# A block of mixing, attention and eight experts: the second norm before the router's ranking, one token tile scaled on VectorE, four slots for hidden tiles

## The chip, the cores and the metric

The kernel runs on one core of a Trainium2 chip. The metric is the device time in microseconds (us) of one execution; the figure for a kernel is the median of its runs. Engines: TensorE (PE; PEld is its weight load), VectorE (DVE), ScalarE (ACT), GpSimd (POOL), SyncE (SP, which only issues DMAs here).

## What is computed

For each of 8 batches: an attention-free mixing layer over 256 image tokens, 128 embedded text tokens appended, relative-position attention over all 384 tokens, then 8 experts weighted by a router. The reference, cut to what matters here:

```python
h = tok_mix(x)                    # h = (h - mu) * rsqrt(var + 1e-5) * ln_g + ln_b at its end
h = jnp.concatenate([h, W_E[x_txt] * sqrt(256)], axis=1)          # 256 + 128 tokens of 256
h = h + attn(_layernorm(h))       # 16 heads of 16, relative positions in a window of 4
x2 = _layernorm(h)
inh = sigmoid(x2 @ Wr / temperature)                              # router, 8 experts
w = exp(-dist / 0.1) * in_zone                                    # dist = |inh - 1/e|
fb = exp(-dist / 0.3); fb_w = normalise(fb * (fb is one of the two largest))
w = normalise(where(sum(w) < 1e-8, fb_w, w))
hidden = silu(x2 @ Wg[e]) * (x2 @ Wu[e])                          # 256 wide, each expert e
out = h + sum_e w[e] * (hidden @ Wd[e])
```

## The kernel before

**Tiles and loop.** Tokens stand on the 128 partitions: three tiles of 128 tokens (two of the image, one of the text), 256 values each. The experts of batch b-1 run in the same iteration as the mixing and the attention of batch b. The first iteration (batch 0) has no experts, seven iterations (six in a loop, one written out after it) have both, and a last pass has the experts of batch 7 alone.

**The order of the work.** `schedule` (line 332) writes out one list of steps, and each engine runs the part that it has in each step, in that order; engines wait for each other with counting semaphores only. So a step that waits on an engine holds up all that stands behind it on that engine. The steps of the mixing and the attention are fixed; between them `fill(n)` puts the next n *units* of the experts, TensorE work of batch b-1. `FILL_MIX` (line 80) says after which step of the mix how many units follow, `FILL_MAXIMA` the same for the 24 maxima (one unit after every third), `FILL_NEGATE` (3 units) for the second negation of the maxima, `FILL_OUT` for the steps behind attention.

**Units.** Gate G(n) and up U(n), n = 0 to 15, two per expert, are six matmuls of 128x384 each (line 913) into one PSUM bank each. ScalarE makes silu of G(n) (line 1070), VectorE multiplies it by U(n) into the hidden tile H(n) (line 1362); U(n+1) may start only when H(n) has freed the bank, and the silu of G(n+1) only when H(n) has read the one before. The hidden tiles have three slots: H(n) goes to slot n mod 3 and waits for the down product that last read it. The down product D(e) of expert e has two parts (line 934): token tiles 0 and 1, then tile 2; VectorE accumulates them, weighted by the router, as A(e) (line 1374), three instructions. The next expert's part waits for the accumulation of the same tiles. H and A don't follow their unit at once on VectorE: each is written just ahead of the next unit, so behind whatever steps lie between.

The units were listed G0 U0 G1 U1, then per expert e: G and U of slot 2e+2, D(e), G and U of slot 2e+3. D(e) has therefore one hidden tile in hand beyond those it reads.

**The mix's end.** The steps in order, with their units: `residual`, `mix_in`, `turn_x2`, `mix_sums`, `router` G0, `mix_out`, `router_zone` U0, `mix_norm` G1, `router_rank` U1 G2, `norm_stats` U2 D0 (first part), `router_pick` D0 (second), `turn_norm` G3 U3, `project_qk`, `project_rel` G4, `project_v` and 15 more units, up to D3.

- `mix_norm`: VectorE normalises the two image tiles out of PSUM into `hid` (line 1115); GpSimd multiplies each by `ln_g` and adds `ln_b` (lines 1439, 1441), tile 0 and then tile 1, counting `hid_ready`.
- `router_rank`, `router_pick`: VectorE, 5 and 11 small instructions, each of which waits for the one before (lines 1331 to 1335, 1341 to 1353).
- `norm_stats`: VectorE waits for `hid_ready` to reach 5 (text tile 1, image tiles 2 each), then takes statistics of the three tiles (lines 1104, 1109); GpSimd's `root` (lines 1405, 1408) turns the variance into 1/sqrt.
- `turn_norm`: VectorE normalises (line 1115, `scratch<-hid`), TensorE transposes (line 658), ScalarE copies (line 977). `project_qk` (line 741) waits for that. Afterwards GpSimd adds a bias to all of `hid` (line 1451).
- From `project_qk` on, ScalarE and VectorE split queries and keys into three bfloat16 parts; SP sends them through DRAM and back in stacked form (lines 561, 566), and last fetches the skewed relative logits as `band_t` (line 595). The first of the maxima (lines 779, 787, reduced on VectorE at line 1220) waits for `band_t`, through a copy on VectorE (line 1214).

**Behind the mix.** The maxima are negated in two halves: TensorE transposes into the bank that tile 2 of a down product also uses, so it waits for the accumulations before it; then attention (scores line 827, band added by VectorE line 1241, exponential by ScalarE line 1033, values line 844). ScalarE loads its table anew between silu and exponential. After attention, `turn_outputs` and `turn_attn`, then `turn_weights`: VectorE scales the relative weights (line 1261), TensorE transposes them (line 658).

## Time and profile before

| | us |
|---|---|
| runs of the kernel before: median (lowest to highest of 3) | 1249.13 (1246.06 to 1252.84) |
| the profiled execution: its own time | 1249.12 |
| its span in the profile | 1247.3 |
| TensorE busy | 1020.4 |
| VectorE busy | 753.0 |
| ScalarE busy | 451.2 |
| GpSimd busy | 247.8 |

The span runs from the first to the last instruction recorded. Busy time counts matmuls as pipelined, with ends that are modelled. "Idle before" in a timeline is the time that the engine did nothing ahead of an instruction, with the instruction that ended last among those it waited for. Times in a timeline are us from the start of the span. The rows are of the iteration whose mix ends at about 490 us; the others of the seven repeat it.

### The profile page before, as it was taken

The numbers are of one execution on the slowest core, as the hardware profiler recorded it, in microseconds if no ns is written. First come the engines' busy times: TensorE is split into PE (matmuls) and PEld (weight loads), VectorE is DVE, ScalarE is ACT, GpSimd is POOL, SyncE is SP. The second block draws the span as 40 slices with busy tenths as digits, with TensorE's granted clock in tenths as the row PEclk, the third lists the DMA queues.
The fourth block names the chain that finished last, engine by engine and source line by source line (L and its number), as shares of the span: only waits on it lengthen the run. The fifth ranks groups of instructions, "written<-read, shape, count | busy, mean of one in ns | idle before, by whom it ended". The sixth has DMA issues, their size and how long they took to land.

```text
span 1247.3 us, 16776 instructions
## 1 busy us (share of the span) xinstructions
PE 1020.4 (82%) x5668; PEld 744.4 (60%) x5668; DVE 753.0 (60%) x1597; ACT 451.2 (36%) x651; POOL 247.8 (20%) x262
## 2 busy tenths in 40 slices
PE   3536698888898798888898798988988888987798
PEld 2412277636786287745786377854876367862687
DVE  7347355774648755685658745685567746487343
ACT  1133512453124723355124622346224531347211
POOL 6228411021200402013200412004120212004000
PEclk9569789989999999999999999999999999999899
DMA  4286203602062110802044020722026020620100
GB/s 110 101 240 174 68 5 97 140 11 53 4 178 59 24 42 33 202 10 39 18 121 115 9 56 0 202 44 39 18 79 157 10 52 5 179 60 18 35 1 13
DMA packets 96962, 87.87 MB, mean 70 GB/s; under 512 B 67281, under 2 KB 85074, under 8 KB 95090
## 3 DMA queue, kind: packets, MB, share of 16 engines
q1 hardware_dynamic: 96524, 86.24, 28.3%
q0 software_dynamic: 384, 1.05, 0.3%
q8 instruction: 17, 0.28, 0.1%
q14 instruction: 37, 0.30, 0.1%
HBM read 60.35 MB, written 26.92 MB: 70 GB/s over the span
## 4 chain that ended last, share of the span: by engine, by line
PE 46%; issue 22%; DVE 17%; DMA 5%; ACT 4%; POOL 4%; SPq 2%; POOLq 0%; DVEq 0%; ACTq 0%
PE S L913 16%; PE S L934 8%; DVE maxima L1220 4%; PE S L844 4%; PE S L779 4%; PE S L827 4%; PE S L741 3%; DVE S L1241 3%; ACT scratch L1033 3%; PE S L658 1%; DMA txt_row<-in_L_txt_W_E,txt_idx 1%; DVE res L1374 1%; PE S L760 1%; SPq L566 1%; PE S L787 1%
## 5 line engine op out<-in xcount | busy, mean ns | idle before, releaser
L1491 POOL TENSOR_TENSOR bands<-scratch,one 64x432 f32<-64x432 f32 x128 | 119.1, 931 | 525.0 <-ACT scratch L1033 519.4
L1070 ACT ACTIVATE silu<-S 128x384 f32<-128x384 f32 x128 | 63.0, 492 | 352.2 <-PE S L913 243.6
L1220 DVE TENSOR_REDUCE maxima<-S 128x2 f32<-128x768 f32 x192 | 172.2, 951 | 19.0 <-PE S L787 17.6
L934 PE MATMUL S<-w_d,hT 128*128 128x256 f32 x768 | 182.0, 382 | 1.5 <-DVE hT L1362 0.7
L1241 DVE TENSOR_TENSOR S<-S,bands 64x144 f32<-64x144 f32 x384 | 154.3, 402 | 43.3 <-PE S L827 32.6
L1033 ACT ACTIVATE scratch<-S 128x768 f32<-128x768 f32 x192 | 154.8, 812 | 56.3 <-DVE S L1241 43.0
L779 PE MATMUL S<-k_st,q_st 128*128 128x384 bf16 x384 | 101.9, 334 | 68.0 <-DVE maxima L1220 39.7
L934 PEld LDWEIGHTS S<-w_d,hT 128*128 128x128 f32 x768 | 143.4, 191 | 22.2 <-issue 2.3
L1362 DVE TENSOR_TENSOR hT<-silu,S 128x384 f32<-128x384 f32 x128 | 70.7, 552 | 116.7 <-PE S L913 97.4
L827 PE MATMUL S<-q_st,k_st 128*128 128x384 bf16 x384 | 98.8, 356 | 40.2 <-ACT scratch L1033 36.7
L1011 ACT ACTIVATE scratch<-scratch 128x816 bf16<-128x816 bf16 x56 | 92.3, 1694 | 41.5 <-DMA scratch<-d_band_t 41.5
L779 PEld LDWEIGHTS S<-k_st,q_st 128*128 128x128 bf16 x384 | 37.6, 98 | 116.3 <-DVE maxima L1220 58.0
L1374 DVE SCALAR_TENSOR_TENSOR res<-S,wgt,res 128x256 f32<-128x256 f32 x168 | 75.5, 479 | 48.0 <-PE S L934 47.7
L827 PEld LDWEIGHTS S<-q_st,k_st 128*128 128x128 bf16 x384 | 25.6, 99 | 132.1 <-ACT scratch L1033 104.0
L844 PE MATMUL S<-scratch,v_one 128*17 128x384 f32 x768 | 84.0, 522 | 12.4 <-ACT scratch L1033 12.3
L913 PE MATMUL S<-x_hi,wu_hi 128*128 128x384 f32 x256 | 72.1, 363 | 23.7 <-DVE hT L1362 23.7
L787 PE MATMUL S<-scratch,ident_b 128*128 128x132 bf16 (+1 forms) x384 | 85.7, 224 | 0.0
L913 PE MATMUL S<-x_hi,wg_hi 128*128 128x384 f32 x256 | 78.1, 386 | 0.0
L658 PE MATMUL S<-ident,scratch 128*128 128x128 f32 (+1 forms) x196 | 30.2, 294 | 51.5 <-DVE scratch L1115 29.9
L913 PE MATMUL S<-x_lo,wu_hi 128*128 128x384 f32 x256 | 66.4, 341 | 0.0
L913 PE MATMUL S<-x_hi,wg_lo 128*128 128x384 f32 x256 | 66.4, 341 | 0.0
L913 PE MATMUL S<-x_lo,wg_hi 128*128 128x384 f32 x256 | 66.3, 340 | 0.0
(167 smaller groups left out, 1515.6 us busy)
## 6 DMA issues: line engine op xcount, KB each, us to landing
bands<-d_band_s SPq DMA_DIRECT2D x16, 864.0 KB, 9.4
scratch<-d_band_t SPq DMA_DIRECT2D x8, 1632.0 KB, 9.6
d_parts<-scratch SPq DMA_DIRECT2D x48, 192.0 KB, 1.9
q_st<-d_parts SPq DMA_DIRECT2D x48, 192.0 KB
k_st<-d_parts SPq DMA_DIRECT2D x48, 192.0 KB
d_band_w<-bands SPq DMA_DIRECT2D x32, 240.0 KB, 3.9
out<-scratch SPq DMA_DIRECT2D x8, 384.0 KB, 2.6
x_in<-in_x SPq DMA_DIRECT2D x8, 256.0 KB, 3.6
```

The source lines that it names most:

```text
L779: pe.matmul(S[:, bank, PAD:PAD + T], q_st[:, h, i * P:(i + 1) * P], k_st[:, h, :], start=True, stop=False, skip_group_check=True)
L787: mm = pe.matmul(S[rows, bank, at + w0:at + w1], ident_b[rows, rows], band_h[rows, i, h, w0:w1], start=False, stop=True, skip_group_check= ...
L827: mm = pe.matmul(S[:, 2 * (n % 3) + l, PAD:PAD + T], k_st[:, h, i * P:(i + 1) * P], q_st[:, h, :], start=True, stop=True)
L844: mm = pe.matmul(S[32 * l:32 * l + VC, 6 + g % 2, 0:T], v_one[:, i, h, :], p_t[:, h % PTS, i, :], start=(i == VALUE_TILES[0]), stop=(i == ...
L913: mm = pe.matmul(dst[:, 0:T], ws[:, e, k, m * P:(m + 1) * P], xs[:, k, :], start=(j == 0), stop=(j == 3 * KT - 1))
L934: mm = pe.matmul(D[:, i // 2, (i % 2) * E:(i % 2 + 1) * E], hT[:, (FT * e + m) % 3, i * P:(i + 1) * P], w_d[:, e, m, :], start=(m == 0), s ...
L1011: nc.scalar.activation(band_h[:, :, heads], band_t[:, :, :, heads].rearrange("p i w h -> p i h w"), ACT.Copy).then_inc(band_turned.sem, 1)
L1033: nc.scalar.activation(dst, S[:, c0:c0 + 2, PAD:PAD + T], ACT.Exp).then_inc(exp_done.sem, 1)
L1220: dve.tensor_reduce(dst, S[:, c0:c0 + 2, PAD:PAD + T], AX, ALU.max).then_inc(max_done.sem, 1)
L1241: dve.tensor_tensor(win, win, band, ALU.add).then_inc(sc_add.sem, 1)
L1374: dve.scalar_tensor_tensor((out_st if last else res)[:, i], D[:, i // 2, (i % 2) * E:(i % 2 + 1) * E], wgt[:, i, e:e + 1], res[:, i], ALU. ...
L1491: nc.gpsimd.tensor_tensor(bands[rows, :, :, 2 * pair:2 * pair + 2].rearrange("p i w h -> p h i w"), win, one[rows].unsqueeze(2).unsqueeze( ...
```

## The change

The steps at the mix's end become: `mix_norm` G1, `norm_stats` U1 G2 U2, `turn_norm` G3, `router_rank` U3, `router_order`, `router_pick` D0 (both parts), `project_qk`, `project_rel` G4 U4, `project_v` and 14 more units. `router_rank` keeps its first two instructions, `router_order` is the other three. Image tile 1 is multiplied by `ln_g` and has `ln_b` added on VectorE, right behind the normalisation; GpSimd does tile 0 alone. The hidden tiles have four slots, and four pairs of gate and up come ahead of the first down product; then per expert D(e) and two pairs. So the units behind `project_v` end with U9 instead of D3, and the units between the maxima are, in order, the parts of D3, G10, U10, G11, U11 and the parts of D4, where they were G9, U9, G10, U10, the parts of D4, G11, U11. The units at the second negation are G12 U12 G13 instead of G12 U12 and the first part of D5. Behind attention come U13, D5, G14, U14, G15, U15, D6, and D7 with its first part after the relative weights are turned; before, the order was the second part of D5, G13, U13, G14, U14, D6, G15, U15, and then D7 likewise.

```diff
...
@@ -78,9 +79,9 @@
-            ("mix_out", 0), ("router_zone", 1), ("mix_norm", 1), ("router_rank", 2),
-            ("norm_stats", 2), ("router_pick", 1), ("turn_norm", 2), ("project_qk", 0),
-            ("project_rel", 1), ("project_v", 15)]
+            ("mix_out", 0), ("router_zone", 1), ("mix_norm", 1), ("norm_stats", 3), ("turn_norm", 1),
+            ("router_rank", 1), ("router_order", 0), ("router_pick", 2), ("project_qk", 0),
+            ("project_rel", 2), ("project_v", 14)]
@@ -168,7 +169,7 @@
-        hT = sb("hT", [P, 3, T])
+        hT = sb("hT", [P, HSLOTS, T])
@@ -266,7 +267,7 @@
-        hid_ready = sig("hid_ready", 5)
+        hid_ready, hid_second = sig("hid_ready", 3), sig("hid_second", 2)
@@ -315,13 +316,15 @@
-        units = [("gate", 0), ("up", 0), ("gate", 1), ("up", 1)]
+        units = []
+        for n in range(HSLOTS):
+            units += [("gate", n), ("up", n)]
         for e in range(NE):
-            if e + 1 < NE:
-                units += [("gate", 2 * e + 2), ("up", 2 * e + 2)]
-            units += [("down", e, 0), ("down", e, 1)]
-            if e + 1 < NE:
-                units += [("gate", 2 * e + 3), ("up", 2 * e + 3)]
+            parts_e = [("down", e, 0), ("down", e, 1)]
+            n = FT * e + HSLOTS
+            if n < FT * NE:
+                parts_e += [("gate", n), ("up", n), ("gate", n + 1), ("up", n + 1)]
+            units += parts_e
...
@@ -932,7 +935,7 @@
-                                       hT[:, (FT * e + m) % 3, i * P:(i + 1) * P], w_d[:, e, m, :],
+                                       hT[:, (FT * e + m) % HSLOTS, i * P:(i + 1) * P], w_d[:, e, m, :],
@@ -1147,6 +1150,13 @@
             def mix_norm(b):
                 norm(b, mix_dve, mix_root, mixed, lambda i: hid[:, i], IT)
+                if not later(b):
+                    dve.wait_ge(loaded[1], 16 * N_LOADS[1])
+                dve.wait_ge(mix_dve.sem, mix_dve.at(b, 5 + 3 * IT))
+                dve.tensor_tensor(hid[:, 1], hid[:, 1], ln_g[:], ALU.mult).then_inc(hid_second.sem, 1)
+                dve.wait_ge(hid_second.sem, hid_second.at(b, 1))
+                dve.tensor_tensor(hid[:, 1], hid[:, 1], ln_b[:], ALU.add).then_inc(hid_second.sem, 1)
@@ -1179,7 +1189,8 @@
             def norm_stats(b):
-                dve.wait_ge(hid_ready.sem, hid_ready.at(b, 5))
+                dve.wait_ge(hid_ready.sem, hid_ready.at(b, 3))
+                dve.wait_ge(hid_second.sem, hid_second.at(b, 2))
                 stats(b, ln2, 0, lambda i: hid[:, i], TT)
@@ -1330,6 +1341,12 @@
                 low = earlier[:].unsqueeze(1).broadcast_to([P, TT, NE, NE])
                 step(dve.tensor_tensor(rpair, other, own, ALU.is_equal))
                 step(dve.tensor_tensor(rpair, rpair, low, ALU.mult))
+            def router_order(b):
+                step = stepper(b, [R_DIST + 7])
+                other = fb.unsqueeze(2).broadcast_to([P, TT, NE, NE])
+                own = fb.unsqueeze(3).broadcast_to([P, TT, NE, NE])
                 step(dve.tensor_tensor(rpair, rpair, rpair2, ALU.add))
                 step(dve.tensor_reduce(rank, rpair, AX, ALU.add))
@@ -1356,10 +1373,10 @@
             def hidden(f, n):
-                if n >= 3:
-                    dve.wait_ge(down_pe.sem, down_pe.at(f, 2 * ((n - 3) // FT + 1)))
-                dve.tensor_tensor(hT[:, n % 3], silu[:], U[:, 0:T], ALU.mult).then_inc(h_done.sem, 1)
+                if n >= HSLOTS:
+                    dve.wait_ge(down_pe.sem, down_pe.at(f, 2 * ((n - HSLOTS) // FT + 1)))
+                dve.tensor_tensor(hT[:, n % HSLOTS], silu[:], U[:, 0:T], ALU.mult).then_inc(h_done.sem, 1)
...
@@ -1412,7 +1429,7 @@
             def mix_in(b):
                 if later(b):
-                    pool.wait_ge(hid_ready.sem, hid_ready.at(b - 1, 5))
+                    pool.wait_ge(hid_ready.sem, hid_ready.at(b - 1, 3))
@@ -1434,11 +1451,10 @@
-                for i in range(IT):
-                    pool.wait_ge(mix_dve.sem, mix_dve.at(b, 5 + 2 * IT + 1 + i))
-                    nc.gpsimd.tensor_tensor(hid[:, i], hid[:, i], ln_g[:], ALU.mult).then_inc(hid_ready.sem, 1)
-                    pool.wait_ge(hid_ready.sem, hid_ready.at(b, 2 + 2 * i))
-                    nc.gpsimd.tensor_tensor(hid[:, i], hid[:, i], ln_b[:], ALU.add).then_inc(hid_ready.sem, 1)
+                pool.wait_ge(mix_dve.sem, mix_dve.at(b, 5 + 2 * IT + 1))
+                nc.gpsimd.tensor_tensor(hid[:, 0], hid[:, 0], ln_g[:], ALU.mult).then_inc(hid_ready.sem, 1)
+                pool.wait_ge(hid_ready.sem, hid_ready.at(b, 2))
+                nc.gpsimd.tensor_tensor(hid[:, 0], hid[:, 0], ln_b[:], ALU.add).then_inc(hid_ready.sem, 1)
             def norm_stats(b):
```

`HSLOTS` is 4. The hunks left out enter `router_order` in the lists of steps.

## Rows read from the trace of the kernel before

**Rows 1.** The page: span; busy time by engine

```profile
span 1247.3 us, 16776 instructions
...
PE 1020.4 (82%) x5668; PEld 744.4 (60%) x5668; DVE 753.0 (60%) x1597; ACT 451.2 (36%) x651; POOL 247.8 (20%) x262
```

**Rows 2.** Waits of TensorE, whole run: us in total, times, longest us

```profile
PE S L913 <- DVE hT L1362: 23.7, 15, 2.6
```

**Rows 3.** TensorE, one iteration: start us, us, line, tiles [idle before <-releaser]

```profile
476.44 0.62 PE L913 MATMUL S<-x_hi,wu_hi 128*128 128x384 f32 x2 [1.54 <-DVE hT L1362]
...
480.30 0.62 PE L913 MATMUL S<-x_hi,wu_hi 128*128 128x384 f32 x2 [1.49 <-DVE hT L1362]
...
486.27 0.88 PE L658 MATMUL S<-ident,scratch 128*128 128x128 f32 x6 [2.06 <-DVE scratch L1115]
...
489.10 2.74 PE L741 MATMUL S<-scratch,w_q 128*128 128x384 f32 x8
```

**Rows 4.** Timeline of VectorE, same iteration

```profile
475.84 0.54 DVE L1362 TENSOR_TENSOR hT<-silu,S 128x384 f32<-128x384 f32 x1
...
480.16 1.07 DVE L1104 BATCH_NORM_STATS2 stat<-hid 128x6 f32<-128x256 f32 x3
...
485.16 1.05 DVE L1115 TENSOR_SCALAR scratch<-hid,mv,rstd 128x256 f32<-128x256 f32 x3
```

**Rows 5.** Timeline of GpSimd (POOL), same iteration

```profile
475.55 0.72 POOL L1439 TENSOR_TENSOR hid<-hid,ln_g 128x256 f32<-128x256 f32 x1 [0.66 <-DVE hid L1115]
...
476.35 0.90 POOL L1441 TENSOR_TENSOR hid<-hid,ln_b 128x256 f32<-128x256 f32 x1
...
486.29 1.87 POOL L1451 TENSOR_TENSOR hid<-hid,bo_all 128x768 f32<-128x768 f32 x1 [3.49 <-DVE scratch L1115]
```

**Rows 6.** Two lines of VectorE, whole run: ns min/median/max

```profile
L1332 DVE TENSOR_TENSOR scratch<-scratch,earlier x8: 358/784/787, 186.5 to 1187.5; 128x192 f32<-128x192 f32 x8
...
L1206 DVE TENSOR_TENSOR v_one<-S,bv_all x24: 411/416/420, 65.5 to 1073.3; 128x256 f32<-128x256 f32 x24
```

**Rows 7.** Timelines of ScalarE and TensorE where the first maxima wait

```profile
516.78 1.67 ACT L1011 ACTIVATE scratch<-scratch 128x816 bf16<-128x816 bf16 x1 [3.10 <-DMA scratch<-d_band_t]
...
517.97 0.34 PE L779 MATMUL S<-k_st,q_st 128*128 128x384 bf16 x1 [1.18 <-DVE scratch L1214]
```

**Rows 8.** Chain that ended last, maxima pass: start us, us, what

```profile
523.49 1.10 PE S L913 x6
...
533.17 1.78 PE S L934 x8
...
544.95 0.49 PE S L658 x3
```

**Rows 9.** Timeline of ScalarE, end of the maxima, first exponential

```profile
547.05 1.28 ACT L1033 ACT_TABLE_LOAD   x1
...
551.09 1.67 ACT L1033 ACTIVATE scratch<-S 128x768 f32<-128x768 f32 x2 [2.76 <-DVE S L1241]
```

**Rows 10.** Timelines of VectorE and TensorE, end of the iteration

```profile
585.88 1.35 DVE L1374 SCALAR_TENSOR_TENSOR res<-S,wgt,res 128x256 f32<-128x256 f32 x3 [1.12 <-PE S L934]
...
588.65 0.82 PE L658 MATMUL S<-ident,scratch 128*72 128x128 f32 x6
```

**Rows 11.** Timeline of TensorE, last pass

```profile
1191.78 0.82 PE L913 MATMUL S<-x_hi,wu_hi 128*128 128x384 f32 x2 [2.60 <-DVE hT L1362]
...
1240.96 2.86 PE L934 MATMUL S<-w_d,hT 128*128 128x256 f32 x12 [0.70 <-DVE hT L1362]
```

**Rows 12.** Busy us by stretch; last three columns: granted clock, DMA share, GB/s

```profile
486.30:490.00 3.70, 3.70 (x21) 3.37 (x22) 0.30 (x1) 1.37 (x3) 1.86 (x1) 1.00 0.00 0
...
1191.80:1197.00 5.20, 5.20 (x19) 4.64 (x19) 1.08 (x3) 0.49 (x1) 0.00 (x0) 0.67 0.00 0
```

**Rows 13.** Timeline of VectorE, first iteration

```profile
47.40 1.08 DVE L1104 BATCH_NORM_STATS2 stat<-hid 128x6 f32<-128x256 f32 x3 [2.73 <-POOL hid L1441]
...
50.09 1.06 DVE L1115 TENSOR_SCALAR scratch<-hid,mv,rstd 128x256 f32<-128x256 f32 x3 [1.26 <-POOL rstd L1408]
```

More of the change, by code:

```diff
@@ L37 @@
 KT = E // P
+HSLOTS = 4
 TXT = 128
@@ L357, in schedule @@
                 fill(3)
-                steps += [("router_zone",), ("router_rank",), ("router_pick",)]
+                steps += [("router_zone",), ("router_rank",), ("router_order",), ("router_pick",)]
                 fill(len(left))
@@ L414, in schedule @@
             return steps
-        LATE_STEPS = ("residual", "turn_x2", "router", "router_zone", "router_rank", "router_pick",
+        LATE_STEPS = ("residual", "turn_x2", "router", "router_zone", "router_rank", "router_order", "router_pick",
                       "gate", "up", "down", "hidden", "accumulate", "store")
@@ L1383, in _ @@
                          "turn_x2": turn_x2, "router": router, "router_zone": router_zone,
-                         "router_rank": router_rank, "router_pick": router_pick,
+                         "router_rank": router_rank, "router_order": router_order, "router_pick": router_pick,
                          "hidden": hidden, "accumulate": accumulate})
```

## The prediction

> **What bounds the kernel now.** The page comes first: the span is 1247.3 us and TensorE is busy for 82% of it [rows 1], so the time is TensorE's work and the gaps in it. The profiled execution took 1249.12 us, 1.8 more than its span; the median of the three runs is 1249.13, so a difference worked out on the trace is added to 1249.1 as it is. The table of waits says which gaps the change aims at: TensorE waited 23.7 us, in 15 places, for a hidden tile of VectorE [rows 2], two places in each of the seven iterations in which the experts of one batch run beside the mixing and attention of the next, and one in the last pass. TensorE's own timeline of one such iteration shows them: 1.54 us before U1 (the up product of slot 1) and 1.49 before U2, then 2.06 before the transposes of the normalised tokens [rows 3], 5.09 in all. VectorE's timeline shows why: H0 and H1, the products that free TensorE's bank, stand behind the router's ranking, and the second norm, at 485.16, does too [rows 4].
>
> What ends a gap is not yet what ends the stage. The projections, at 489.10 [rows 3], start a chain of DMAs whose last, the bands, lands at 516.78; TensorE has been idle for 1.18 us when the first maxima start at 517.97 [rows 7]. So that stage is set by the DMA chain, and only what brings the projections forward shortens it.
>
> **The stage of the mix, part by part.** The first norm ends on VectorE just before 475.84, where H0 starts now [rows 4]. Two instructions are put in between, a multiplication and an addition over 128x256. Alone each should take 0.42 (the nearest row of that size, with one operand in PSUM) [rows 6]. But GpSimd multiplies and adds the other tile at that moment, from 475.55 on [rows 5], and VectorE's two-operand instruction of 128x192, 0.36 at its fastest, has a median of 0.78 [rows 6]; the fastest is the last pass, where GpSimd is idle. So I let the two take turns: the multiplication waits until about 476.1, GpSimd's addition is pushed and done at about 477.0, VectorE's addition ends at 477.4. H0 starts there, 1.56 later than now, U1, which follows H0 by 0.60 [rows 3, 4], at 478.0, and the gap before it grows from 1.54 to 3.1. The bounds: 0.9 later if the engines do not hinder each other, 1.9 if each waits for the whole of the other's instruction.
>
> That last bound is a rule of the Trainium skill (SBUF — State Buffer, section "Who interferes with whom"): an instruction of VectorE with both inputs in SBUF and one of GpSimd that reads SBUF exclude each other, and whichever starts first keeps the shared ports for its whole length. The trace bears out the turns; read to the letter the rule would put H0 at 477.7 and add about 2 us to the forecast over seven iterations.
>
> What this buys: GpSimd now ends its tile at about 477.15 and no longer does the second, so the statistics, at 480.16 now [rows 4], start behind H0 at 477.9. The norm follows its statistics by 2.69 where nothing else is in the way [rows 13], so it starts at 480.6 and ends at 481.65, for 485.16 plus 1.05 [rows 4]. TensorE from U1 to the projections takes 489.10 - 476.44 = 12.66 now, of which 1.49 and 2.06 are gaps [rows 3]; about 0.5 more are tails of matmuls that overlap the next one where no gap follows (estimate), which leaves 8.6. The units in that stretch are the same after the change. From 478.0 that is 486.6, and 0.3 is still lost, as U2 is through at 481.3 and the norm at 481.65. The projections start at 486.9, **2.2 us earlier** (1.8 to 2.8 by the bounds above).
>
> The ranking and the picking move behind H2. Their steps cost nothing there as long as something covers them: they wait for GpSimd's 1.87 (the bias added to the hidden state) [rows 5] and end at about 488, with H3 and the first accumulation behind them on VectorE; H3 is wanted by U4 at about 494.6 and VectorE by the splitting of the queries at about 491. If they took 3 us more, each further microsecond would delay that splitting, and so SP's whole chain of DMAs. No DMA is added. SP's issues stay in order and move with the projections; GpSimd's gather of text rows waits for a count that is long reached. The fourth slot and the split of the ranking in two cost no instruction.
>
> **What is late next.** The bands land at 514.6 instead of 516.78. TensorE is there earlier still, since D3 (the down product of expert 3, first part 1.78 [rows 8]) leaves this stretch and G9 and U9 (1.10 each [rows 8]) come in: its gap grows, nothing is gained beyond 2.2. D3 turns up in the maxima pass, between whose reductions a unit is put every third item. There the order becomes D3, D3, G10, U10, G11, U11, D4, D4 for G9, U9, G10, U10, D4, D4, G11, U11. TensorE's unit sits in the loop from one reduction to the next, so a first down part costs 1.78 - 1.10 = 0.68 more than a gate: 0.68 for D3's, 0.68 for D4's at its new place, and -0.30 where D4's was (VectorE, with H10 and a negation there, doesn't let all of it go). The second parts are short, but two accumulations, 0.45 each [rows 10], push the reduction after them: +0.26 for D3's, -0.17 for D4's old place. Last, D4 now ends the pass, and the second negation, at 544.95 [rows 8], needs D4's bank: after the last reduction all three accumulations, 1.35, come first: +1.13. Together 0.68 + 0.68 - 0.30 + 0.26 - 0.17 + 1.13 = **+2.3**.
>
> After the negation G13 (1.10) stands in place of D5's first part (1.78), and no accumulation holds VectorE when attention starts. But G13's activation comes ahead of ScalarE's table load of 1.28 [rows 9], so the first exponential, at 551.09 [rows 9], comes only **0.5 earlier** than the negation alone would have it.
>
> Behind attention the 0.68 is paid back (+0.6), and D6 now runs directly ahead of the turned relative weights: VectorE makes these after D6's first accumulations, which it begins 1.9 after D6 starts, while now they are made under G15 and U15, with the transposes at 588.65 behind them [rows 10]: +0.7 of wait, less 0.4 for H15, which no longer delays D7. **+0.9.**
>
> **The sum without the clock.** Per iteration -2.2 + 2.3 - 0.5 + 0.9 = +0.5, seven times +3.5. The first iteration has no experts: there GpSimd's four instructions stand alone in front of the statistics (2.73 idle [rows 13]), and two of them leave: -1.1. In the last pass the 0.70 before the last down product [rows 11] goes, but D7 then waits for D6's accumulations: -0.4. Sum +2.0: 1251.1.
>
> **The clock.** TensorE ran at full clock (1.00) behind the gap of 2.06, and at 0.67 of it on average, partly at 1.2 GHz, in the 5.2 us behind the gap of 2.60 of the last pass [rows 3, 11, 12]. The new gap of 3.1 is longer than that. A fall would make U1 to U2 slower: in the last pass 5.2 us at 0.67 lost about 1.7, of which the 0.3 that TensorE waits anyway is free, and not all of a fall need meet work: 1.2 per fall (estimate). It may come in none of the iterations (0, if the gap stays near 2.4, the lower bound) or in all seven (+8.4). The one gap of this size was followed by a fall, but it was one; I take half, **+4** (3.5 x 1.2). The forecast is 1249.1 + 2.0 + 4.0 = **1255**, 0.5% above, which is about what a measurement of this kernel can tell from no change.
>
> **The rivals.** *Slower by more (chance 0.39).* The wait on H0 takes the place of those removed: the clock falls behind the 3.1 us gap in every iteration, and U1, G2 and U2 run on the slow clock. For it: [rows 11, 12]; against it: it needs the gap to stay above some 2.5 us. Time: 1251.1 + 8.4 = 1259.5; with a second fall behind the longer gap ahead of the maxima, in half the iterations, some 1264. It decides from about 5 falls in seven. The Trainium skill (TensorE: Matmul & The Clock Gate, section "What's actually happening") has the throttled clock as the default that activity releases; the trace agrees with its 0.67, and by that rule alone the time would be that of this rival.
>
> *Faster (0.18).* The maxima pass absorbs D3 and D4, because its reductions on VectorE and not the units on TensorE set its pace, and the three accumulations fit ahead of the negation: then +2.3 is about 0.5, and each iteration comes to -2.2 + 0.5 - 0.5 + 0.9 = -1.3. Time: 1249.1 - 9.1 - 1.5 = 1238.5. Against it: in the chain that ended last the units stand between the reductions [rows 8]. It decides once the pass grows by less than 1.2.
>
> *No contention (part of the middle 0.43).* VectorE's two instructions take 0.84 beside GpSimd, the gap is 2.4, the clock stays: 1251.1 - 7 x 0.6 = 1247, the same as before within what can be told.
>
> **How the numbers follow.** Within 0.5% (1242.9 to 1255.4) lie the sum without the clock, up to three or four falls, and the case without contention: 0.43. Above it the first rival, 0.39; below it the second, 0.18. The forecast lies at the upper edge of the middle case. The range 1238 to 1264 reaches to both rivals and leaves out a tenth on either side.
>
> **What would show it.** TensorE's gap before U1 at about 3.1, none before U2, 0.3 before the transposes; VectorE's two new instructions at 0.5 to 0.9 instead of 0.42; GpSimd with two fewer per iteration; the projections 2.2 earlier against the same iteration's first norm; the maxima pass, from the first maxima to the second negation, 26.98 now [rows 7, 8], at about 29.2; stretches of granted clock 0.5 behind U1 in some iterations. The prediction is wrong if H0 starts before 476.9 or if the maxima pass does not grow.

## The result and the profile after

The changed kernel took 1267.24 us (median; 1265.54 to 1268.73) against 1249.32 of the kernel before in the same comparison: a ratio of 1.0136, with a 95% interval of 1.0106 to 1.0166. It is slower by 1.4%, where 1255 was forecast and 1264 was the upper end of the range.

The page of the kernel after, its span, busy time and the row of the bands' transfer (the last number is the median from issue to landing; the same row of the kernel before has 9.6):

```profile
span 1263.5 us, 16772 instructions
...
PE 1033.3 (82%) x5668; PEld 758.4 (60%) x5668; DVE 756.5 (60%) x1613; ACT 449.7 (36%) x651; POOL 234.6 (19%) x246
...
scratch<-d_band_t SPq DMA_DIRECT2D x8, 1632.0 KB, 10.4
```

Against [rows 1] the span grew by 16.2 us, and TensorE's busy time by 12.9 with the same 5668 instructions: the same work ran on a lower clock for longer (mean 0.939 for 0.952). GpSimd (POOL) has 16 instructions fewer, two for each batch, and VectorE 16 more, as the change says. The bands, which the prediction left alone, take 0.8 us longer to land.

TensorE's waits after (us in total, times, longest us):

```profile
PE S L916 <- DVE hT L1379: 22.0, 8, 3.2
...
PE S L661 <- DVE scratch L1272: 9.4, 8, 6.7
PE S L661 <- DVE res L1391: 8.2, 6, 1.4
```

The wait for a hidden tile came 15 times for 23.7 us [rows 2]; it comes 8 times for 22.0 now: in six of seven iterations one wait of about 3 us has taken the place of two of 1.5. The two rows below it are waits of the new order of units: the relative weights wait behind D6's accumulations (seven times; the eighth, of 6.7, was there before, as 6.5), and the second negation behind D4's.

TensorE in the mix of one iteration after, the one of the fifth batch, to be read beside [rows 3]:

```profile
622.25 0.51 PE L916 MATMUL S<-x_hi,wg_lo 128*128 128x384 f32 x2
625.80 1.01 PE L916 MATMUL S<-x_hi,wu_hi 128*128 128x384 f32 x2 [3.05 <-DVE hT L1379]
626.61 0.84 PE L916 MATMUL S<-x_lo,wu_hi 128*128 128x384 f32 x2
...
631.73 0.82 PE L661 MATMUL S<-ident,scratch 128*128 128x128 f32 x6
...
637.09 2.74 PE L744 MATMUL S<-scratch,w_q 128*128 128x384 f32 x8
```

The gap before U1 is 3.05, and behind it a pair of matmuls takes 0.84 where it took 0.51 before the gap. The gaps before U2 and before the transposes are gone here. The second is gone only because TensorE is so slow that VectorE is always done first: in the iteration whose clock stays whole at this place, U2 follows G2 without a gap too, and 0.21 us is left before the transposes:

```profile
189.75 0.87 PE L661 MATMUL S<-ident,scratch 128*128 128x128 f32 x6 [0.21 <-DVE scratch L1118]
```

VectorE at the same place, beside [rows 4]:

```profile
622.79 0.99 DVE L1118 TENSOR_SCALAR hid<-S,mv,rstd 128x256 f32<-128x256 f32 x2 [0.63 <-POOL rstd L1425]
623.82 0.60 DVE L1157 TENSOR_TENSOR hid<-hid,ln_g 128x256 f32<-128x256 f32 x1
624.46 0.83 DVE L1159 TENSOR_TENSOR hid<-hid,ln_b 128x256 f32<-128x256 f32 x1
625.21 0.54 DVE L1379 TENSOR_TENSOR hT<-silu,S 128x384 f32<-128x384 f32 x1
625.67 1.07 DVE L1107 BATCH_NORM_STATS2 stat<-hid 128x6 f32<-128x256 f32 x3
```

The two new instructions take 0.60 and 0.83, and H0 (625.21) follows them; the statistics follow H0 at once instead of waiting for GpSimd.

The granted clock of the mix (from 5 us behind the first norm's statistics to the projections) in three of the eight iterations; the columns are those of [rows 12], the clock is the third number from the end:

```profile
185.90:195.15 9.25, 8.84 (x48) 8.21 (x49) 8.07 (x27) 2.35 (x5) 2.93 (x3) 1.00 0.00 0
333.68:344.01 10.33, 10.15 (x48) 9.82 (x49) 7.43 (x30) 2.35 (x5) 2.89 (x3) 0.83 0.00 0
...
625.63:637.09 11.46, 11.29 (x48) 10.88 (x49) 7.35 (x30) 2.35 (x5) 2.89 (x3) 0.73 0.00 0
```

Of the seven iterations with experts one has a clock of 1.00 here, two 0.83 or 0.84, and four 0.73 or 0.74. The six that fall are those with a gap of 3.05 to 3.19 us before U1. In the remaining one, the first row, the clock was already at 0.50 ahead of this stretch (174.30 to 184.60), G1 ended late, and the gap is 1.34. The kernel before has 1.00 in six of the seven and this in one, the matmuls being slow from behind the gap of 2.02 ahead of the transposes on:

```profile
332.86:345.68 12.82, 9.32 (x43) 8.33 (x43) 8.00 (x29) 1.85 (x4) 3.96 (x5) 0.87 0.00 0
```

**Where the 16.2 us came from.** Marks read from the timelines cut each of the seven iterations into stages, and the differences to the kernel before, summed over the seven, tell where the time lies: the mix (first statistics to projections), the bands (projections to the first maxima), what lies behind (first maxima to the output projection), and all the rest of the span (the first iteration, the last pass, and the stretches from an output projection to the next first statistics). Here they are with the runs that are told below (us of the profiled executions):

| kernel | mix | bands | behind | rest | span |
|---|---|---|---|---|---|
| after | -4.8 | +4.9 | +19.4 | -3.4 | +16.2 |
| GpSimd scales both tiles (1) | -3.9 | -0.1 | +18.8 | +0.4 | +15.2 |
| scaling behind H0 (1) | -16.5 | +3.8 | +28.1 | -2.7 | +12.7 |
| gap filled (1) | -15.4 | +2.4 | +23.5 | +1.1 | +11.6 |
| three slots (1) | -12.6 | +3.4 | +5.7 | -2.0 | -5.4 |
| one semaphore more, never used (2) | -1.5 | -0.5 | +0.2 | -2.1 | -3.9 |
| slots and order of units alone (2) | -3.6 | -0.5 | +19.3 | -2.0 | +13.1 |
| three slots, scaling behind H0 (2) | -16.5 | +3.2 | +5.8 | -3.9 | -11.3 |
| norm ahead of ranking alone (2) | -8.6 | -0.5 | +7.5 | -2.8 | -4.4 |
| the same, 5 small instructions more (3) | -2.5 | +3.7 | +5.4 | +0.5 | +7.2 |
| three slots, behind H0, 14 small ones in the loop (3) | -16.4 | -0.3 | +0.5 | -0.7 | -16.9 |

The row of the unused semaphore is the kernel before in all that it executes. It shows how far two profiled executions can stand apart with nothing changed: 1.5 us in the mix, a fall of the clock that the trace of before has in one iteration and this run has not, and 3.9 in the span. Differences of that size in the table say nothing by themselves.

### The profile page after: what moved, and what is told of

It is laid out like the page before. It is cut to its first block, busy times and chain, and to the rows that moved or that the text cites. A ratio compares the mean times of both kernels' runs of the same rounds, so it can differ in the third digit from the quotient of the medians.

```text
span 1263.5 us, 16772 instructions
## 1 busy us (share of the span) xinstructions
PE 1033.3 (82%) x5668; PEld 758.4 (60%) x5668; DVE 756.5 (60%) x1613; ACT 449.7 (36%) x651; POOL 234.6 (19%) x246
## 4 chain that ended last, share of the span: by engine, by line
PE 35%; issue 24%; DVE 15%; DMA 9%; SPq 5%; ACT 5%; POOL 4%; POOLq 0%; DVEq 0%; ACTq 0%
PE S L916 11%; PE S L937 6%; DMA scratch<-d_band_t 6%; DVE maxima L1231 5%; SPq L569 4%; PE S L847 4%; PE S L830 4%; ACT scratch L1036 3%; PE S L744 3%; PE S L782 3%; DVE S L1252 2%; PE S L661 1%; DVE res L1391 1%; DMA x_in<-in_x 1%; DMA w_d<-in_L_ffn_Wg 1%
## 5 line engine op out<-in xcount | busy, mean ns | idle before, releaser
L1231 DVE TENSOR_REDUCE maxima<-S 128x2 f32<-128x768 f32 x192 | 171.5, 950 | 28.1 <-PE S L790 28.0
L937 PEld LDWEIGHTS S<-w_d,hT 128*128 128x128 f32 x768 | 143.4, 191 | 20.2 <-issue 0.7
L847 PE MATMUL S<-scratch,v_one 128*17 128x384 f32 x768 | 83.2, 518 | 12.4 <-ACT scratch L1036 12.3
L916 PE MATMUL S<-x_lo,wu_hi 128*128 128x384 f32 x256 | 69.4, 354 | 0.0
L916 PE MATMUL S<-x_hi,wu_lo 128*128 128x384 f32 x256 | 69.2, 353 | 0.0
```

Of the source, the lines that this page charges most:

```text
L847: mm = pe.matmul(S[32 * l:32 * l + VC, 6 + g % 2, 0:T], v_one[:, i, h, :], p_t[:, h % PTS, i, :], start=(i == VALUE_TILES[0]), stop=(i == ...
L916: mm = pe.matmul(dst[:, 0:T], ws[:, e, k, m * P:(m + 1) * P], xs[:, k, :], start=(j == 0), stop=(j == 3 * KT - 1))
L937: mm = pe.matmul(D[:, i // 2, (i % 2) * E:(i % 2 + 1) * E], hT[:, (FT * e + m) % HSLOTS, i * P:(i + 1) * P], w_d[:, e, m, :], start=(m == ...
L1231: dve.tensor_reduce(dst, S[:, c0:c0 + 2, PAD:PAD + T], AX, ALU.max).then_inc(max_done.sem, 1)
```

## First experiments: the gap or the units

Two theories were put up. **A**: the gap of 3.05 us ahead of U1 lowers the clock in each iteration, and most of the loss comes from there. **B**: the loss comes from the new order of the units behind the mix, D3 and D4 between the maxima and D6 ahead of the turned weights. (The times of this group stand against 1246.44 us of the kernel before.)

**GpSimd scales both tiles again**, the rest as after:

```diff
-                dve.tensor_tensor(hid[:, 1], hid[:, 1], ln_g[:], ALU.mult).then_inc(hid_second.sem, 1)
...
-                dve.tensor_tensor(hid[:, 1], hid[:, 1], ln_b[:], ALU.add).then_inc(hid_second.sem, 1)
...
+                for i in range(IT):
...
```

> Undoes one part: GpSimd scales both image tiles again, order of the steps, units and four slots as after the change. Theory A (the clock): the gap of 3.05 us before U1, made by VectorE's two instructions ahead of H0, lowers TensorE's clock in every interleaved iteration and that is most of the loss. Then here the gap before U1 is about 1.5 again, no half-clock stretch follows it, the projections start about 1 us earlier than before the change, and the time is 1259 to 1263. Theory B (the units): the loss is made behind the mix, by D3 and D4 between the maxima and by D6 ahead of the turned weights, and the clock hardly counts: then the time stays at 1266 to 1270, as the statistics come later than after the change.

Measured: 1268.91 us, ratio 1.0187 (1.0112 to 1.0262), from runs that lie wide apart, 1259.34 to 1277.67. Where the clock of the mix stays whole the projections come after 15.10 us instead of 16.33, and the iteration takes 143.8 us, little more than before's 143.4. But in the first three iterations with experts the clock falls, in the mix or behind it, and they take 145.8 to 149.9; in the seventh it falls too. So the time does not tell A from B here, but taking the scaling away from VectorE did not make the kernel faster.

**VectorE's scaling moved behind H0**, so that the gap before U1 is 1.54 us again:

```diff
             def mix_norm(b):
...
-                dve.tensor_tensor(hid[:, 1], hid[:, 1], ln_g[:], ALU.mult).then_inc(hid_second.sem, 1)
...
             def norm_stats(b):
...
+                dve.tensor_tensor(hid[:, 1], hid[:, 1], ln_g[:], ALU.mult).then_inc(hid_second.sem, 1)
...
```

> Moves one part: VectorE's multiplication and addition of image tile 1 stand behind H0 instead of ahead of it, nothing else differs from after the change. Theory A: U1 starts as early as before the change, gap about 1.5, no half-clock stretch behind it, the projections 2.2 to 2.4 us earlier than before the change, time 1249 to 1254 (what remains is lost behind the mix). Theory B: the clock hardly counts, time 1262 to 1268.

Measured: 1262.04 us, ratio 1.0126 (1.0094 to 1.0157): the time that B gave, with the mix that A gave. The stretch of the mix and the first 3.5 us of the maxima in the fifth batch's iteration:

```profile
624.36:633.51 9.15, 7.78 (x42) 6.84 (x42) 7.84 (x27) 1.86 (x4) 2.90 (x3) 1.00 0.00 0
...
663.10:666.60 3.50, 3.31 (x14) 1.96 (x15) 2.14 (x3) 3.50 (x3) 0.00 (x0) 0.53 0.24 36
```

The mix has the whole clock in all seven iterations, and the projections come 2.18 us earlier than before (14.15 us behind the first statistics for 16.33). But now the clock is halved at the start of the maxima, in five of the seven iterations, where the kernel after has it in two. The sums say how much came back: the mix gains 11.7 us on the kernel after (-16.5 for -4.8), and what lies behind loses 8.7 of them (+28.1 for +19.4).

**The gap filled**: 14 matmuls without use into a free bank between G1 and U1.

```diff
+                if n == 1:
+                    for j in range(N_WARM):
+                        pe.matmul(O[:, 0:T], wg_hi[:, 0, 0, 0:P], x2_hi[:, 0, :], start=True, stop=True)
                 hidden_tile(f, n, U, wu_hi, wu_lo, up_pe, h_done)
```

> Adds work: 14 matmuls of 128x384 whose result is not used, into a bank that is free at that point, between G1 and U1, where TensorE waits 3.05 us. They do nothing but keep TensorE busy; H0 and U1 start when they did. Theory A: no half-clock stretch behind U1, U1 to the projections 2 us shorter, time 1251 to 1256. Theory B, or another cause of the slow matmuls than the gap: U1, G2 and U2 stay slow, time 1266 or above.

Measured: 1261.33 us, ratio 1.0121 (1.0089 to 1.0152): as the run above, and in neither range. The projections come after 14.3 us, as A said, and the clock falls at the start of the maxima in five of seven (0.75 there in the same iteration).

**Three slots and the units of before**, norm and scaling of after:

```diff
-HSLOTS = 4
+HSLOTS = 3
...
+        units = [("gate", 0), ("up", 0), ("gate", 1), ("up", 1)]
...
```

> Undoes the other part: three slots and the list of units of before, the second norm ahead of the ranking and VectorE's scaling as after the change. Behind the mix the order of units is that of before. Theory A: the half-clock stretches behind U1 stay and the mix gains nothing, the maxima pass and the end of the iteration are as before the change: time 1247 to 1253. Theory B: the whole loss goes and the gain of the mix is left, time below 1243.

Measured: 1243.94 us, ratio 0.9967 (0.9947 to 0.9988): just above B's figure, and faster than the kernel before, though its gap before U1 is that of the kernel after. The clock falls behind it in every second iteration:

```profile
472.30:482.63 10.33, 10.16 (x48) 9.81 (x49) 7.49 (x31) 2.35 (x5) 2.90 (x3) 0.83 0.00 0
617.55:626.79 9.24, 8.86 (x49) 8.22 (x50) 8.04 (x28) 2.35 (x5) 2.89 (x3) 1.00 0.00 0
759.03:769.37 10.34, 10.16 (x49) 9.82 (x49) 7.51 (x31) 2.35 (x5) 2.90 (x3) 0.83 0.00 0
```

The gap is 3.05 us in both kinds of iteration (and in all but the seventh, which has 1.57). TensorE's U1 in the middle one of these three, where the clock stays whole:

```profile
617.72 0.62 PE L914 MATMUL S<-x_hi,wu_hi 128*128 128x384 f32 x2 [3.05 <-DVE hT L1377]
```

So B carries the loss: taking the fourth slot and its order of units away turns +1.4% into -0.3%, while closing the gap, in either way, leaves +1.2%.

## Second: each part alone, and the bands

In this group (against 1246.16 us) the parts of the change stand alone, and a suspicion on the bands is tried: they land some 0.7 us later in every run with the second semaphore.

**One more semaphore, never used**, in the kernel before:

```diff
-        hid_ready = sig("hid_ready", 5)
+        hid_ready, hid_second = sig("hid_ready", 5), sig("hid_second", 2)
```

> The kernel before with one more semaphore declared and never used. In the changed kernel and in every run with the second semaphore the transfers of the bands land some 0.7 us later after the projections than before (10.3 to 10.4 us from issue to landing against 9.6). Theory N (the new semaphore moves the numbers of the later ones and that lengthens the transfers): 10.3 us here, and 7 iterations x 0.65 = 4.5 us more, about 1251 against 1246.4. Theory M (it goes with VectorE's scaling, that is with what runs beside the transfers or when they start): 9.6 us as before, and 1246.4 within 1.5 us.

Measured: 1246.62 us, ratio 1.0016 (0.9992 to 1.0040), the bands after 9.6 us. Theory N fell.

**Four slots and the new order of units alone**, in the kernel before:

```diff
-        units = [("gate", 0), ("up", 0), ("gate", 1), ("up", 1)]
+        units = []
+        for n in range(4):
+            units += [("gate", n), ("up", n)]
...
```

> The kernel before with four slots and the unit order of the change, its norm, its ranking and its fills kept. Theory B (the loss is behind the mix: the down projections between the maxima and ahead of the turned weights): the maxima about 1.9 us longer than 26.98 and the end of the iteration about 1.5 us longer, so about +3.0 us for each of seven iterations, less about 2 us in the last pass and the first iteration: 1263 to 1268. Theory A (the wait of TensorE ahead of U1 and the clock that falls behind it carry the loss): the wait ahead of U1 stays 1.54 us, no half-clock stretch in the mix, and 1246 to 1250.

Measured: 1261.73 us, ratio 1.0107 (1.0076 to 1.0138). TensorE in the fifth batch's iteration, at the second negation and at the relative weights, beside [rows 8, 10]:

```profile
693.35 0.49 PE L660 MATMUL S<-ident,maxima 128*8 128x128 f32 x3 [1.37 <-DVE res L1376]
...
737.86 0.85 PE L660 MATMUL S<-ident,scratch 128*72 128x128 f32 x6 [0.40 <-DVE scratch L1263]
```

The first maxima start at 664.42 there, so the negation comes after 28.93 us, as after and against 26.98 before. It waits 1.37 us for D4's accumulations, and the relative weights wait 0.40 behind D6's: both waits of the change, without its norm and its scaling. The time is a little under B's range, and what lies behind the mix costs as much as in the kernel after (+19.3 for +19.4). This part alone is most of the loss.

**Three slots, scaling behind H0**: the run with three slots and the move of the run with the scaling behind H0, no other edit.

> Three slots and the unit order of before, the norm ahead of the ranking, and VectorE's two scaling instructions behind H0. Theory B with the clock as the smaller share: the projections 2.2 us earlier in each iteration with no half-clock stretch in the mix, the maxima and the end as before, and the bands 0.65 us later: about 2.2 - 0.65 = 1.5 us for each of seven iterations, 1234 to 1238. Theory C (half-clock stretches that are removed in one place come back in another, at the start of the maxima as in the run with the scaling behind H0 and four slots): the maxima about 1 us longer, and 1241 to 1244, as the run with three slots and the scaling ahead of H0.

Measured: 1235.84 us, ratio 0.9899 (0.9872 to 0.9925): B's figure, and a kernel faster than both. The mix is 2.2 us shorter in each iteration; but the clock falls at the start of the maxima in three of seven, so C has a share in it too.

**The norm ahead of the ranking alone**: GpSimd scales both, three slots, the units of before.

```diff
-            ("mix_out", 0), ("router_zone", 1), ("mix_norm", 1), ("router_rank", 2),
-            ("norm_stats", 2), ("router_pick", 1), ("turn_norm", 2), ("project_qk", 0),
+            ("mix_out", 0), ("router_zone", 1), ("mix_norm", 1), ("norm_stats", 3), ("turn_norm", 1),
+            ("router_rank", 0), ("router_order", 0), ("router_pick", 3), ("project_qk", 0),
```

> The kernel before with the second norm ahead of the ranking and nothing else: GpSimd scales both tiles, three slots, the unit order of before. Theory B: the projections 1.2 us earlier in each iteration, as in the run with GpSimd scaling both and four slots (15.10 against 16.33), the bands landing after 9.6 us as before, the maxima and the end as before: 7 x 1.2 = 8.4 us less, 1237 to 1240. Theory C: half-clock stretches come back at the start of the maxima or in attention, and 1242 to 1246. If the scaling on VectorE is what makes the difference at all, the time stays at 1246.

Measured: 1243.03 us, ratio 0.9972 (0.9956 to 0.9989): the figure of C. The mix is shorter by the 1.2 us expected, the bands land after 9.5, and attention gives nearly all of it back: +7.5 over seven iterations, in which the clock from the table load to the last output is 0.89 in all seven where the kernel before has 0.94 in six. The fifth batch's iteration, in this run:

```profile
686.34:716.82 30.48, 24.60 (x155) 6.64 (x154) 20.71 (x51) 21.42 (x28) 14.38 (x16) 0.89 0.03 9
```

The bands' delay is not in this run, and it is in the run before it: what differs is VectorE's scaling.

## Third: what delays the bands

The two runs just told are alike from the projections on: every instruction of TensorE, VectorE and ScalarE up to the landing of the bands stands within 0.03 us of the other's, counted from the projections, and GpSimd is idle. The transfer is issued 18.0 us behind the projections in both, as in the kernels before and after. Yet it takes 9.5 us in the one and 10.2 in the other. What differs is in the queue of instructions. Here are the DMA queues of the run with the norm alone (projections at 628.38) in a stretch from 26.6 us behind the projections on:

```profile
q1 hardware_dynamic: 3422, 0.24, 126.6%
q14 instruction: 1, 0.01, 2.1%
```

A block of instructions is loaded near there once in every round of the loop. In the kernels whose bands take 9.4 to 9.8 us it comes 27.5 to 28.6 us behind the projections, as the bands' last packets go or just after; in those with 10.0 to 10.6 it comes 22.6 to 25.6 us behind them, amid the transfer. The ten kernels so far, six rounds of each, show no exception. VectorE's two instructions would move that place if the block is one of VectorE's program. The Trainium skill (Runtime: NRT & Kernel Launch, section "Instruction fetch mechanics") says that each engine's sequencer fetches its instructions in blocks by a DMA queue of its own, at a cost that is mostly hidden. Here it shows in another transfer, as the next runs tell. (The times of this group stand against 1250.32 us, 4 us more than those of the second group, so ratios and not times are to be compared across the two.)

**Five small instructions on VectorE**, in the run with the norm alone, which scales nothing on VectorE:

```diff
             def project_v(b):
...
+                for j in range(5):
+                    dve.memset(spare[:, 4 + j:5 + j], 0.0)
```

> The run with the norm ahead of the ranking alone, with 5 small instructions on VectorE in the same place; VectorE scales nothing. Theory L: the block of instructions moves from 27 us behind the projections to between 20 and 25, the bands land after 10.2 us instead of 9.5, and the time rises by 6 x 0.6 to about 1246.5. If VectorE's scaling itself lengthens the transfer: 9.5 us and 1243.

Measured: the bands after 10.2 us, as theory L says, with the block in a stretch from 23.5 us behind the projections (634.52) on:

```profile
q1 hardware_dynamic: 185, 0.81, 102.2%
q14 instruction: 1, 0.01, 1.0%
```

One landing of the seven, in the iteration written out behind the loop, takes 10.1 us with the block at 8.5 us; why, stays open. The time was 1256.91 us, ratio 1.0041 (1.0008 to 1.0074), 10 us above what was expected, of which the kernel before accounts for 4 in this group. Against the run without the five, the bands account for 4.2 of 11.6 us of the span, near the 3.6 expected, and the mix for 6.1. That is its clock: two neighbouring iterations of this run, the same instructions, from the first statistics to the projections:

```profile
473.70:490.48 16.78, 14.34 (x61) 12.76 (x61) 12.36 (x42) 2.46 (x5) 6.70 (x9) 0.81 0.00 0
619.41:634.52 15.11, 11.26 (x61) 9.98 (x61) 10.78 (x38) 2.35 (x5) 6.70 (x9) 1.00 0.00 0
```

One has the whole clock, the other 0.81 of it. In five of seven iterations of this run the clock falls in the mix, and in one of seven of the run without the five.

**Fourteen of them inside the loop**, in the run with three slots and the scaling behind H0 (the same edit with 14):

> The same 14 small instructions on VectorE inside the loop, behind the values' projection, where VectorE waits for TensorE. Theory L: the block of instructions comes before 18 us behind the projections, the bands land after 9.5 us instead of 10.2, and 1232 to 1234 (the 14 instructions take under 1 us of VectorE's time and push one hidden tile by about 0.4 us, which the wait for the bands covers). If the lengthening has another cause: 10.2 us and 1236 to 1239.

Measured: 1232.43 us, ratio 0.9858 (0.9824 to 0.9892), the bands after 9.5 us, the block 11 us behind the projections. The 14 instructions themselves took 0.22 us of VectorE:

```profile
631.05 0.22 DVE L1220 MEMSET spare<- 128x1 f32 x14
```

This is the lowest median of the study. Its mix keeps the 2.2 us of the change, its bands are back, and what lies behind gives back 0.5 us over seven iterations.

**Fourteen of them ahead of the loop**, in the preparation:

> The run with three slots and the scaling behind H0, with 14 small instructions on VectorE in its preparation, ahead of the loop over the batches. Theory L (the bands land 0.65 us later where the transfer of a block of instructions falls between 18 and 27 us behind the projections, amid the transfer of the bands; where that block comes is set by how many of VectorE's instructions stand ahead of it): the block of instructions moves from 23 us behind the projections to before 18, the bands land after 9.5 us instead of 10.2, and the time falls by 6 x 0.6 = 3.6 us to about 1232. If the block's place is counted from the loop's own beginning, nothing moves: 10.2 us and 1236.

Measured: 1233.80 us, ratio 0.9876 (0.9853 to 0.9899), the median of the bands 9.5 us, the block 11.6 to 12.3 us behind the projections. So instructions ahead of the loop move its place inside the loop as well. One of six iterations still has 10.3, with the block at 12.3, ahead of the transfer; why, stays open.

**Four slots with the units of before**, in the run with three slots and the scaling behind H0:

```diff
-HSLOTS = 3
+HSLOTS = 4
```

> The run with three slots and the scaling behind H0, with a fourth slot and the unit order of before: the slot without the order. Theory B says that the order of the units carries the loss and not the slot: 1235 to 1237 as with three slots (1235.84), the maxima from 27.6 us. If the slot itself did it (its address, its wait), the maxima would come to about 29.5 us and the time to about 1250.

Measured: 1235.63 us, ratio 0.9891 (0.9868 to 0.9915), as with three slots. The slot costs nothing and brings nothing; the order of the units is what costs.

## Why the prediction was wrong

**Right: the mix without the clock.** H0 was to start 1.56 us later, the gap before U1 to be 3.1, the projections 2.2 earlier. H0 stands 4.58 us behind the first statistics for 3.08 (+1.50) and the gap is 3.05. Where the clock holds behind that gap, in three iterations of the run with three slots, the projections come 14.24 us behind the first statistics for 16.33, 2.1 earlier; with the scaling behind H0 it is 14.15. The two instructions, priced by taking turns with GpSimd, took 1.43 together, against 0.84 without contention (estimate of the prediction, from [rows 6]).

**Right: the units behind the mix.** The maxima pass was to grow by 2.3 and measured +1.95 (666.58 to 695.51 for [rows 7, 8]), with D4's three accumulations ahead of the second negation as told; so the rival in which the pass absorbs D3 and D4 (a growth under 1.2) did not come. The other two terms were off in opposite senses: the first exponential gave back 0.7 of it instead of 0.5 (it comes 34.42 us behind the first maxima for 33.18), attention itself 0.3 more, and the end of the iteration grew by 1.46 instead of 0.9. The size of the end was too small because of a second wait that the prediction did not see. Both, in the fifth batch's iteration of the kernel after:

```profile
734.74 0.61 PE L916 MATMUL S<-x_hi,wg_hi 128*128 128x384 f32 x2 [0.32 <-ACT silu L1073]
...
740.09 0.85 PE L661 MATMUL S<-ident,scratch 128*72 128x128 f32 x6 [0.40 <-DVE scratch L1272]
```

The pair G15 waits 0.32 for a silu of ScalarE, beside the 0.40 of the relative weights. From the first maxima on the prediction had +2.7 an iteration, 18.9 over seven; measured were 19.4, and 19.3 with the units alone.

**Wrong: the bands.** The step "the bands land at 514.6 instead of 516.78", the gain of the projections carried on to the bands in full, counted no DMA as added and so took the landing for fixed. It took 0.7 us longer in each iteration, 4.9 over seven, from an issue that had moved with the projections as told. The runs showed in its place that a landing is late where a block of instructions is loaded amid it, and that small instructions on VectorE alone bring this about (9.5 to 10.2) and undo it (10.2 to 9.5). The prediction counted VectorE's two added instructions at their own time only. Two landings, of 10.1 and 10.3 with no block amid them, remain unexplained.

**Wrong: the clock.** The step "1.2 per fall", "I take half, +4", was too small in count, and in price for most falls. The clock fell in the mix in six of seven iterations. In two of them (clock 0.83) the projections came 15.3 us behind the first statistics for 14.25 with none, a price of 1.1, as forecast. In four (clock 0.73) they came after 16.4 to 16.5, a price of 2.2, and all of the gain was given back. Over seven iterations the mix gained 4.8 instead of the 11.2 forecast (7 x 2.2 - 4.2), and 1.5 of the 4.8 is the one fall that the trace of before has there. What also failed is the rule behind the price: the length of the one gap in that stage. The trace of before held a case against it, one fall behind a gap of 2.02, where the prediction read only an iteration without. The run with three slots had the same gap of 3.05 in six iterations and a fall behind three, and the run with five small instructions, whose longest gap there is 1.76, had falls in the mix of five iterations and none in two, with the same instructions.

Together: mix 6.4 and bands 4.9 worse, what lies behind 0.5; less 1.3 for a last pass that gained 1.7 instead of 0.4, and 0.6 ahead of the first mix. That is 10 us, the distance from the sum of the prediction (+6.2) to the span (+16.2). The last two are of the size that two profiles of one program differ by. The term of the first iteration, -1.1, came out by luck: its mix gained 1.1 as told, but its bands also came 1.2 earlier, and the first statistics of the next iteration 1.4 later. The rival that came out is the first, with the clock falling behind the gap; its 1259.5 to 1264 lacked the bands and the long falls. The signs named at the prediction's end nearly all came true (the projections 2.2 earlier is the exception), but none of them watched the landing of the bands or the length of a fall.

The price of the two engines side by side held. Behind H0, where VectorE's multiplication starts just ahead of GpSimd's addition (622.90 and 622.95 in one iteration), it takes 0.417 us in the median of that run (duration in ns: least, median, most):

```profile
L1189 DVE TENSOR_TENSOR hid<-hid,ln_g x8: 414/417/592, 43.9 to 1063.3; 128x256 f32<-128x256 f32 x8
```

Ahead of H0, where GpSimd had started first (623.42 for 623.82), it took 0.60, and the addition 0.83. The Trainium skill (SBUF — State Buffer, section "Who interferes with whom") has the two engines exclude each other for such instructions; the trace agrees in that the one which starts first keeps its pace, but H0 came 1.50 later and not the 1.9 that the letter of the rule gives.

## What to carry to other kernels

A change of several parts is best priced and run part by part: here the norm's move with VectorE's scaling gained 0.3% (1% with the scaling behind H0), the order of the units lost 1.1%, and a forecast of 0.5% for both together hid that. A fall of the clock behind a gap cost 1.1 us in some iterations and 2.2 in others, so it needs a range and not one price, and the clock that is won in one stage is not won until the stages behind it are measured too. Where a transfer of many packets ends a stage, look at the instruction queue beside it: a few instructions more or fewer on an engine can move a block of its program into the transfer or out of it.

## What was not expected of the hardware

The block of instructions, 0.01 MB, moved amid the bands' 1632 KB, lengthened their landing from 9.5 to 10.2 us; 5 small instructions that write 128x1 each were enough to do so, and 14 (0.22 us in all) enough to undo it. The order went with every late landing but two. How so small a transfer holds up the landing by 0.7 us was not tried.

The halved clock moves rather than goes. With the gap closed (the run with the scaling behind H0) 11.7 us were won in the mix and 8.7 lost behind it, and two neighbouring iterations of one run with the same instructions had clocks of 0.81 and 1.00 in the same stage. What decides between them was not settled here.
